# Layer 1's experts: nine single tiles' weights loaded from DRAM by the sync queue instead of copied by ACT

## The reference, cut to what matters

```python
def _expert_ffn(xf, Wi_e, bi_e, Wg_e, bg_e, Wo_e, bo_e, g_e, b_e):
    h = gelu(xf @ Wi_e + bi_e) * sigmoid(xf @ Wg_e + bg_e)
    r = xf + (h @ Wo_e + bo_e)
    mu, var = mean(r), mean((r - mu) ** 2)
    return (r - mu) * rsqrt(var + EPS) * g_e + b_e

probs = softmax(xf @ Wr + br)
topw, topi = top_k(probs, 2)          # of 8 experts
topw = topw / sum(topw)
out = sum over the two chosen experts of topw * _expert_ffn(xf, ...)
```

## Time and profile before

| | |
|---|---|
| median of 3 runs | 1242.38 us (1239.73 to 1244.12) |
| profiled execution, its own time | 1242.04 us |
| its span | 1240.1 us |
| mean granted TensorE clock | 0.924 |
| PE busy | 1008.7 us, 81% |
| DVE busy | 802.5 us, 65% |
| ACT busy | 788.3 us, 64% |
| POOL busy | 780.1 us, 63% |
| layer 1's experts | from about 988 to 1214 us of the span |

### The profile page before, as it was taken

One profiled execution on the slowest core, in us unless ns is written; L12 is line 12 of the kernel. 1 busy time (PEld: TensorE's weight loads), 2 busy tenths in 40 slices (PEclk: granted clock), 3 DMA queues, 4 the chain that ended last, 5 costly groups with the idle time before them and its releaser, 6 DMA issues. The chain is left out here.

```text
span 1240.1 us, 40089 instructions
## 1 busy us (share of the span) xinstructions
PE 1008.7 (81%) x16123; PEld 807.0 (65%) x16123; DVE 802.5 (65%) x1631; ACT 788.3 (64%) x1729; POOL 780.1 (63%) x807
## 2 busy tenths in 40 slices
PE   6789999999999865698787386899965589999970
PEld 4567777877777754597676143565644579988870
DVE  6578888878878758200001395788966737676775
ACT  5356556556556544686566574677754679988983
POOL 6577687787787520577777312788840068878864
PEclk9889999999999986899999698899987789999995
DMA  4733222323221034311112502000026311111117
GB/s 131 163 63 55 55 55 55 59 51 55 57 53 21 4 92 131 85 53 52 52 52 52 144 1 70 6 6 7 6 16 218 118 54 45 44 45 48 42 32 209
DMA packets 120839, 79.30 MB, mean 64 GB/s; under 512 B 44145, under 2 KB 111121, under 8 KB 120529
## 3 DMA queue, kind: packets, MB, share of 16 engines
q1 hardware_dynamic: 111568, 58.12, 20.6%
q0 software_dynamic: 9088, 18.63, 5.1%
HBM read 58.15 MB, written 17.76 MB: 61 GB/s over the span
## 5 line engine op out<-in xcount | busy, mean ns | idle before, releaser
L2120 ACT ACTIVATE act_x_m<-ps_h_x_m,fc_bias_x_m 128x256 f32<-128x256 f32 (+1 forms) x480 | 185.2, 470 | 66.4 <-PE ps_h_x_m L2059 60.3
L1027 ACT ACTIVATE probT<-ps_t 128x512 f32<-128x512 f32 (+1 forms) x208 | 118.7, 594 | 139.7 <-PE ps_t L855 138.5
L2059 PE MATMUL ps_h_x_m<-x_T_x_m,fc_x_m 128*128 128x256 f32 (+1 forms) x960 | 203.0, 362 | 5.0 <-ACT x_T_x_m L2128 2.8
L2231 POOL DMA_INDIRECT x_rows_x_m<-h_dram,token_m x142 | 140.4, 989 | 96.9 <-POOLq L1754 57.4
L2059 PEld LDWEIGHTS ps_h_x_m<-x_T_x_m,fc_x_m 128*128 128x128 f32 x960 | 165.5, 194 | 24.0 <-issue 6.8
L2078 PE MATMUL ps_o_x_m<-proj_x_m,act_x_m 128*128 128x128 f32 x1136 | 144.7, 280 | 33.7 <-DVE y_x_m L2166 25.6
L2241 POOL DMA_INDIRECT y_dram<-y_x_m,dest_m x142 | 142.0, 1000 | 47.8 <-issue 40.3
L2078 PEld LDWEIGHTS ps_o_x_m<-proj_x_m,act_x_m 128*128 128x128 f32 x1136 | 133.8, 193 | 43.7 <-ACT act_x_m L2120 28.7
L777 POOL TENSOR_TENSOR rel_y<-rel_raw,own_rows 128x1024 f32<-128x1024 f32 x64 | 130.6, 2043 | 21.2 <-ACT rel_raw L1035 21.1
L957 DVE TENSOR_REDUCE neg_max<-ps_s 128x8 f32<-128x512 f32 (+1 forms) x64 | 95.5, 1491 | 65.6 <-PE ps_s L840 65.4
L2166 DVE TENSOR_TENSOR y_x_m<-ps_o_x_m,out_rows_m 128x256 f32<-128x256 f32 (+1 forms) x40 | 15.8, 395 | 164.0 <-DMA y_dram<-y_x_m,dest_m 127.7
(11 more groups left out here) (311 smaller groups left out, 2132.4 us busy)
## 6 DMA issues: line engine op xcount, KB each, us to landing
q_spread<-q_dram SPq DMA_DIRECT2D x256, 64.0 KB
got_m<-y_dram SPq DMA_DIRECT2D x32, 256.0 KB, 5.0
h_dram<-h_rows_m SPq DMA_DIRECT2D x16, 256.0 KB, 2.3
x_rows_x_m<-h_dram,token_m POOLq DMA_INDIRECT x142, 2.6
y_dram<-y_x_m,dest_m POOLq DMA_INDIRECT x142, 2.3
x<-L_attn_x SPq DMA_DIRECT2D x8, 256.0 KB, 4.1
q_dram<-qT SPq DMA_DIRECT2D x8, 256.0 KB, 10.5
gates<-gate_dram SPq DMA_DIRECT2D x16, 128.0 KB, 4.0
```

What stands on the lines that cost most here:

```text
L1027: act.activation(probT[to:to + n, store(m, ch), :, (2 * j + s) % 4, :], ps_t[row:row + n, t % 2, :].rearrange("p (g c) -> p g c", g=GROUPS ...
L2059: m = pe.matmul(ps_h[:, l, g, f % 2, 0:w], fc[:, slot, l, f * P:(f + 1) * P], x_T[:, slot % 2, 0:w], start=True, stop=True)
L2120: m = act.activation(out[:, slot % 2, f, 0:w], ps_h[:, l, g, f % 2, 0:w], ACT.Tanh if l else ACT.Gelu, scale=0.5 if l else 1.0, bias=fc_bi ...
L2231: pool.indirect_dma_start(out=x_rows[:, slot, h, :], out_offset=None, in_=k.h_dram, in_offset=bass.IndirectOffsetOnAxis(ap=r.token[:, c:c ...
```

## The change

In layer 1, the weights and biases of tiles 31 to 39 are not copied by ACT any more. SP reads the number of the tile's expert, waits until the slot of the ring is free (`out_ready`: the second layer of the tile four before is done), and issues four transfers: the two first matrices and the second matrix from DRAM, 256 KB each, and the biases (4 KB) from their table in SBUF. The source's address comes from a register. PE and ACT wait for the sum of the slot's transfers on `w_in` in place of `w_copied`. The loads stand in SP's program ahead of the load of the gates. For the double tiles, and for all of layer 0, ACT copies as before; all experts' matrices are still loaded into SBUF.

```diff
--- before.py
+++ after.py
@@ -1972,7 +1972,6 @@
     nf = len(weights.fc)
     nr = len(weights.rows)
     nw = nf + 2
-    resident = r.resident
     with ExitStack() as ctx:
         def sb(n, s, dt=F32):
             return ctx.enter_context(nc.sbuf_tensor(n + name, s, dt))
@@ -2012,9 +2011,16 @@
         def exists(j):
             return 0 <= j < XTILES
 
-        def count(j):
-
-            return j // UNROLL + 1
+        def fetched(j):
+
+            return gated and PAIR_TILES <= j < XTILES
+
+        def wait_weights(eng, j):
+
+            if fetched(j):
+                eng.wait_ge(w_in[j % UNROLL], 16 * nw * len(range(j, PAIR_TILES - 1, -UNROLL)))
+            else:
+                eng.wait_ge(w_copied, j + 1)
 
         def moved(j, ring=UNROLL):
 
@@ -2027,9 +2033,9 @@
             else:
                 sp.wait_ge(tables_in, 16 * (nf * FK + nr))
 
-            for j in range(0 if resident else XTILES):
+            for j in range(PAIR_TILES, XTILES if gated else PAIR_TILES):
                 s = j % UNROLL
-                wait(sp, out_ready, j - UNROLL + 1)
+                sp.wait_ge(out_ready, j - UNROLL + 1)
                 e = sp.value_load(r.expert[0:1, j:j + 1], min_val=0, max_val=E - 1)
                 for f, (w, _) in enumerate(weights.fc):
                     sp.dma_start(fc[:, s, f, :], w[bass.ds(e, 1), :, :].rearrange("o p f -> (o p) f")).then_inc(w_in[s], 16)
@@ -2047,10 +2053,7 @@
         def _(pe):
             def first_layer(n):
                 slot, w = n % UNROLL, P * halves(n)
-                if resident:
-                    pe.wait_ge(w_copied, n + 1)
-                else:
-                    pe.wait_ge(w_in[slot], 16 * nw * count(n))
+                wait_weights(pe, n)
                 pe.wait_ge(x_copied, n + 1)
                 for g in range(2):
                     for l in range(nf):
@@ -2099,17 +2102,15 @@
                 act.activation(proj[:, s, :, :].rearrange("p f c -> p (f c)"), r.proj[:, bass.ds(e, 1), :, :].rearrange("p o f c -> p (o f c)"),
                                ACT.Copy).then_inc(w_copied, 1)
 
-            if resident:
-                act.wait_ge(r.weights_in, 16 * E * (nf + 1))
-                act.wait_ge(tables_in, 16 * (nf * FK + nr))
-                if gated:
-                    act.wait_ge(halved, 1)
-                copy_weights(0)
-                copy_weights(1)
+            act.wait_ge(r.weights_in, 16 * E * (nf + 1))
+            act.wait_ge(tables_in, 16 * (nf * FK + nr))
+            if gated:
+                act.wait_ge(halved, 1)
+            copy_weights(0)
+            copy_weights(1)
             for n in range(-1, XTILES + 1):
                 if exists(n):
-                    if resident:
-                        act.wait_ge(w_copied, n + 1)
+                    wait_weights(act, n)
                     slot, w = n % UNROLL, P * halves(n)
                     for g in range(2):
                         for l in range(nf):
@@ -2126,7 +2127,7 @@
                     act.wait_ge(x_turned, n + 1)
                     wait(act, fc_ready, 2 * nf * (n - 1))
                     act.activation(x_T[:, n % 2, 0:P * halves(n)], ps_x[:, 0:P * halves(n)], ACT.Copy).then_inc(x_copied, 1)
-                    if resident and exists(n + 1) and n >= 1:
+                    if exists(n + 1) and n >= 1 and not fetched(n + 1):
                         copy_weights(n + 1)
 
         @block.vector
```

## The result

The changed kernel has a median of 1237.83 us against 1242.62 us, 20 runs each: ratio 0.996, 95% interval 0.9945 to 0.9976. Two of its 20 runs were slow, at 1899.89 and 2446.84 us, and the ratio is without them. Two later comparisons, of the same kernel (12 runs each) against new runs of the one before, gave 0.9979 (0.9956 to 1.0003) and 0.9985 (0.9968 to 1.0001). The first shows it faster by 3 to 7 us; the other two point to about 2 us, but their intervals reach no change. The forecast was 1.8.

The account below looks back on a forecast made before the run. POOL over the double tiles, then DVE, were taken to bound the experts, not ACT. Terms -1.6-0.2=-1.8 us took the profiled 1242.04 us to 1240.2, cost of added loads hidden; range 1237.5 to 1243.8.

Parts of the forecast that it names:

- Term -1.6: Start of layer 1's experts: first gathers freed of the gates' load, first turn 1.63 us earlier; bounds 0 and -3.9.
- Slowed and not blocked: First gathers: DMA engines alternate between queues, so the gates' load delayed the gathers 1.6 us while itself taking 5.9.
- Term -0.2: DVE's residual of tile 38: its 0.23 us wait for the second layer goes with ACT early; bounds 0 and 5.1.
- ACT's 5.1 us as slack: Nine weight copies off ACT, 0.57 us each, 5.1 in all: nearly all slack, as POOL, then DVE, leads.
- A load of 6.3 us: SP's weight load per tile, 0.3+1.3+4.7 us: hidden, by 1.1 us at tile 39, the tightest, and more before.
- rivals 3 and 4: Late weights, last tiles: 8 to 9.5 us a load, 1240.8 to 1242.3, chance 0.12; 11 or more, 1246.7, 0.06.
- The gates at the end: Gates requested behind tile 39's weights, landing near 1207, SP next wanted at 1214.05: hidden by seven microseconds, cost nothing.

Follow-up runs that it names:

- gates_late: Kernel before with only the gates' load moved behind the end of tile 35, ACT still copying all weights; run twice: 1.0004 and 0.9978, experts 223.8 us both.
- gates_first: Changed kernel with layer 1's gates requested ahead of the loop over the nine tiles: 1.000 of the kernel before, experts 226.8 us.
- sp_lands: Changed kernel with SP waiting after each tile's four transfers until they have landed: one run, 1245.57 us, experts 236.4 us.
- release_late: Changed kernel with each of the nine loads released one tile later: 1.0118 of the kernel before, experts 240.2 us.
- all_sp: Changed kernel with SP loading the weights of layer 1's tiles 2 to 39, ACT copying only tiles 0 and 1: 0.9996 of before, experts 226.2 us.
- short: Kernel before, ACT copying everything, gates' load moved behind tile 35, POOL gathering nine tiles ahead, its layer 1 constant set after the first gather: 0.9987, experts 224.3 us.
- half_gather: Changed kernel without the second gather of double tiles 8 to 30, so computing something else: 0.9951 of the kernel before, experts 218.9 us.

## Why the prediction was right, and where it was off

**The mechanism was right.** The gain is the gates' load leaving the first gathers' way, not the copies leaving ACT. gates_late has it alone and gives all of the shorter phase; gates_first has the rest alone and gives nothing. The time came in the range, 0.3 us above its lower end and outside the forecast's own 1238.8 to 1241.6; the medians of the two repeats, 1241.87 and 1241.43, lie near the middle. So the first number says little on the terms. 0.3%, the bound set for telling a change, lies inside the measured interval, so between "faster" and "the same" the measurement barely decides, and the first comparison alone came out on the faster side.

**Term -1.6, mis-sized.** It should have been about 2.5, in two parts. Layer 0's step of 2.81 us was the measure; layer 1 with nothing ahead of its first gathers makes it in 2.45 to 2.60 over ten profiles, and the turn comes 1.9 us earlier in the phase. The other 0.6 the prediction had at nothing: tile 0's first layer runs partly at the lower granted clock (0.50 in the windows at its start, 1.00 at its end), and it takes 6.20 to 6.49 us in the three profiles with a load ahead of the gathers and 5.35 to 5.56 in the ten without. So tile 1's turn and its power come 2.5 us earlier, and with them the unbroken chain. Why the clock rises sooner behind the shorter wait wasn't tested. I had named layer 0's small loads beside its gathers as a doubt only in the other direction.

**Slowed and not blocked: a wrong reading.** The prediction took the 1.6 us against the gates' 5.9 as a sign that the gathers shared the DMA engines with the gates. The gates had 4.0 of their 5.9 us left when the second gather was issued, and the turn came 4.44 after it, so these numbers didn't tell. The packets do: none of a gather ran before the gates were nearly through, and in gates_first too, none before 995.5 with the gates requested at 991.33. The sum doesn't change by it.

**Term -0.2, right in place and in size, but not visible in the whole.** The wait is gone, and from tile 39's first gate to the read of `y_dram` it is 10.01 to 10.05 us in the three profiles of the changed kernel, against 10.32, 10.32 and 10.35 in before and the two of gates_late. The phases agree within 0.3 us all the same, since the double tiles scatter by as much: tile 10's power, long before the first load, comes 81.6 to 81.7 us after the halving in the changed kernel's three profiles and 81.3 in gates_late's two. That this is scatter and not the change is shown by sp_lands and release_late, with the changed kernel's code up to there: 81.4 and 81.2. One profile doesn't fit: gates_first has no wait and 10.32.

**ACT's 5.1 us as slack: right for this kernel only.** gates_first and all_sp show it worth nothing. short shows that it isn't slack by nature: with the phase 1.4 us shorter by POOL's ninth gather, 2.0 us of it count. The prediction said that ACT was caught up with only at the last tiles; that margin was thinner than the wording suggests. The Trainium skill's rule (Perfetto Trace Analysis, Identifying the Most-Contended Engine) to optimise first what is busiest would have gone to ACT at 10.00 of 10; the runs gave the time to POOL, at 8.19. Over the double tiles, where half_gather relieves POOL, its share is lower than ACT's too: 46.95 against 53.34 of 58 us from 1060 to 1118 in the kernel before.

**A load of 6.3 us: right in size, wrong about the tightest tile.** Measured were 6.0 alone and 7.4 at tile 36. That the sum is so near is partly luck: the read of the expert's number takes SP with the wait 0.75 us, not 0.3, and issues and landing together took 5.26, not 6.0; the 4.7 taken as the middle of the landings was neither their median, 5.8, nor halfway between 3.1 and 7.5. I had worked out the budget for tiles 35 and 39 and assumed the rest in between; PE's only wait was at tile 36, 0.6 us, on no path that counts. The prices of rivals 3 and 4 don't agree either. By the prediction's own working tile 36's weights hold tile 35's second layer (1193.31), and so tile 39's load, as soon as a load takes more than 1193.31-2.0-1183.0=8.3 us, not 10.6; at 9.5 us that is 1183.0+9.5+3.2+9.5-1201.86=3.3 us at tile 39, and not 2.1. The range still held it, and release_late shows that such waits come together with a slower first layer.

**The gates at the end: right.** Requested at 1190.05, behind tile 39's weights, 16.6 us before SP's next read; gates_late's experts are no shorter for having no weights ahead of them.

**What stays open.** The traces account for 2.3 to 2.6 us. The first comparison said 4.8 (its interval 3.0 to 6.8), the two repeats 2.6 and 1.9. Since executions differ by up to 15 us before the changed code begins, I hold the excess for spread, but that is argued from the repeats, not shown.

## What to carry to other kernels

Where a program's early part scatters more than an edit is worth, cut the phase out between two instructions of the trace and compare that: here it repeats within 0.3 us when whole times disagree by 0.3%. An effect of 0.3 us wants a shorter piece still. A busy engine earns nothing while another leads; but slack found this way belongs to one balance of the kernel, and the next improvement may use it up. Before a phase that starts with small gathers on the critical path, look at what else is requested in that microsecond, above all what is wanted only much later.

## What was not expected of the hardware

A wait of PE can cost more than its length. In release_late, first layers behind waits of 2.5 to 3.4 us ran 1.4 to 1.8 us longer than the same instructions elsewhere (3.36 to 3.78 against 2.0), with the granted clock at 0.57 in one window over such a layer. Behind its waits of 1.2 and 1.7 us, and behind the one of 0.6 us in the changed kernel, they took 2.05.

A load of 1 MB on SP's queue, requested just ahead of POOL's first gathers, kept their packets off the DMA engines until it was nearly done: 1760 of its 2064 packets ran first, and the turn that wants the rows came 1.9 us later in the phase.

The DMA engines carried the weights beside POOL's gathers and scatters without lengthening them: in all_sp at 184 GB/s over the double tiles (1060 to 1118; 46 in the kernel before), the powers, with two gathers and two scatters between them, stayed 5.80 us apart.
